# Opposite 64x64 corners for the join of a block inverse, with operands of two batches moved by DMA and the third projection placed ahead

## The reference, cut to what matters

```python
q = _causal_conv_silu(hidden_states @ Wq, conv_q)   # k, v alike, 16 heads, DK 96, DV 192
def step(S, inp):
    q_t, k_t, v_t, g_t, b_t = inp
    S = S * jnp.exp(g_t)[..., None, None]
    kv = jnp.einsum('bhk,bhkv->bhv', k_t, S)
    delta = (v_t - kv) * b_t[..., None]
    S = S + jnp.einsum('bhk,bhv->bhkv', k_t, delta)
    o = jnp.einsum('bhk,bhkv->bhv', q_t, S)
    return (S, o)
_, o = jax.lax.scan(step, S0, xs)
```

## Time and profile before

| | us |
|---|---|
| median of 3 runs | 2243.75 |
| lowest and highest | 2242.56, 2245.61 |
| the profiled execution, own time | 2241.96 |
| its span, first to last instruction | 2240.1 |

### The profile page before, as it was taken

How to read it: one execution, slowest core, us unless ns; L and a number is a source line. 1 busy time by engine, 2 the same in 40 slices (tenths; PEclk the granted TensorE clock), 3 DMA queues, 4 the chain that set the end, 5 groups by cost and what they waited for, 6 DMA issues and landing times. The chain is left out here.

```text
span 2240.1 us, 58394 instructions
## 1 busy us (share of the span) xinstructions
PE 2135.4 (95%) x21560; PEld 1489.9 (67%) x21560; DVE 1987.2 (89%) x4323; ACT 1373.8 (61%) x3891; POOL 1069.0 (48%) x1539
## 2 busy tenths in 40 slices
PE   5899999999999999999999999999999998868998
PEld 3576767676777776777767777767676766743544
DVE  8999999999999999999999999999999986467786
ACT  5566666666666667666766767666656554214655
POOL 2545454544545454545454545454545352125554
PEclk8999999999999999999999999999999998788999
DMA  5223333333333333334344433432222222140000
GB/s 143 51 69 80 78 82 80 85 84 85 85 80 85 74 84 90 94 87 94 89 94 92 95 91 95 93 76 66 66 62 51 58 51 55 28 164 9 20 24 29
DMA packets 455176, 169.16 MB, mean 76 GB/s; under 512 B 378310, under 2 KB 433894, under 8 KB 454380
## 3 DMA queue, kind: packets, MB, share of 16 engines
q1 hardware_dynamic: 454892, 165.43, 30.8%
HBM read 83.30 MB, written 56.90 MB: 63 GB/s over the span
## 5 line engine op out<-in xcount | busy, mean ns | idle before, releaser
L1491 DVE SCALAR_TENSOR_TENSOR d_y<-bank,d_cw,d_y 128x508 f32<-128x508 f32 (+2 forms) x576 | 421.3, 732 | 6.7 <-ACT d_y L1253 1.7
L851 POOL TENSOR_SCALAR d_ms<-d_sso 128x4 f32<-128x4 f32 x64 | 14.5, 226 | 531.6 <-ACT d_junk L1392 531.6
L799 POOL TENSOR_TENSOR d_Gm<-cst,gh 128x512 f16<-128x512 f32 x128 | 130.9, 1044 | 189.0 <-DVE d_ohl L1658 184.5
L1260 ACT ACTIVATE d_th<-d_y 128x512 f32<-128x512 f32 x192 | 121.0, 630 | 150.2 <-DVE d_y L1497 123.6
L1253 ACT ACTIVATE d_y<-bank,d_cw 128x512 f32<-128x512 f32 x192 | 130.7, 681 | 56.0 <-PE bank L917 53.7
L1664 DVE SCALAR_TENSOR_TENSOR x<-bank,x 128x512 f32<-128x512 f32 x128 | 87.0, 680 | 83.4 <-PE bank L1064 83.4
L834 POOL TENSOR_TENSOR d_V<-d_tok,d_kinv 128x640 f32<-128x640 f32 (+1 forms) x128 | 137.7, 1096 | 46.5 <-issue 44.0
L881 POOL TENSOR_SCALAR d_K<-d_tok,d_Em 128x96 f32<-128x96 f32 x256 | 155.9, 624 | 0.1
L1302 ACT ACTIVATE d_tok<-bank 128x384 f32<-128x384 f32 x256 | 125.5, 490 | 41.5 <-PE bank L933 37.7
L1382 ACT ACTIVATE d_Dl<-bank 128x384 f32<-128x384 f32 x128 | 62.2, 490 | 119.2 <-PE bank L1040 119.1
L1028 PE MATMUL bank<-d_wgh,hhi 128*128 128x192 f16 x1024 | 126.6, 246 | 0.0
(11 more groups left out here) (337 smaller groups left out, 6618.6 us busy)
## 6 DMA issues: line engine op xcount, KB each, us to landing
normed<-d_ohl SPq DMA_DIRECT2D x64, 384.0 KB, 3.7
lt_blocks<-d_LT SPq DMA_DIRECT2D x64, 256.0 KB, 2.6
d_fw<-turned_gate_w SPq DMA_DIRECT2D x32, 256.0 KB, 3.2
d_XT<-x_blocks SPq DMA_DIRECT2D x128, 64.0 KB, 2.4
d_X<-x_blocks SPq DMA_DIRECT2D x128, 64.0 KB, 2.5
d_fw<-turned_val_w SPq DMA_DIRECT2D x32, 256.0 KB, 3.2
d_fw<-turned_out_w SPq DMA_DIRECT2D x32, 256.0 KB, 2.8
d_st<-in_L_attn_Wg_dram SPq DMA_DIRECT2D x16, 384.0 KB, 4.1
```

The lines of the kernel that those rows point to most:

```text
L799: nc.gpsimd.tensor_tensor(Gm[:, w, :, :], over(U, 1, B), over(gh[:, w, n, :], 2, P), ALU.mult).then_inc(s["Gm_ready"], 1)
L1260: nc.scalar.activation(th[:, :, :], y[(st.p + j) % 2][:, :, :], ACT.Tanh).then_inc(s["tanh_done"], 1)
L1491: nc.vector.scalar_tensor_tensor(out=yy[:, :, tap:], in0=pp[:, :, 0:P - tap], scalar=cw[:, ds(st.kp, 1), t, 3 - tap], in1=yy[:, :, tap:], ...
```

## The change

- `y_join` and `x_join` do four matmuls of 64 rows and 64 columns each in place of four of 128 rows. Batches 0 and 1 use array rows 0 to 63 and write PSUM partitions 64 to 127; batches 2 and 3 use rows 64 to 127 and write partitions 0 to 63 (for `x_join` the other way round). The two kinds alternate in the instruction order. `x_join` writes the last quarter of bank 3.
- Operands of batches 2 and 3 are needed on the other 64 partitions. Three DMAs of 32 KB on SyncE's queue bring them in every step: LJ (from LT, `turned_join`), and XJ's two halves (from X and XT, `halves`).
- `turned_join` stands before `gather`, `halves` between `next_weights` and `store`. `y_join` waits for LJ and the first half of XJ, `x_join` for the second.
- `proj(2)` moves ahead of `y_join`: five of six parts for c > 0 (the sixth between the joins), all six for c = 0, with `turn(2)` among them. At c = 0 one output tile and `turn(3)` stand between the joins where there is one output unit; in steps 0, 4 and 60 nothing does.
- ScalarE copies the upper XT block first in `copy_x64`, `copy_yj` copies 128 partitions x 128 in place of 64 x 256, `join` is two copies of 64 x 128 in place of one of 64 x 256.

```diff
+            def turned_join(n, q):
+                past(sp, "x21_done", n)
+                past(sp, "LT_ready", B * n + B)
+                sp.dma_start(LJ[HB:P, :, :], LT[q][0:HB, 2:B, HB:P]).then_inc(s["LJ_in"], 16)
+            def halves(n):
+                past(sp, "X_ready", 7 * n + 5)
+                sp.dma_start(XJ[HB:P, :, :], X[0:HB, 0, 2:B, :]).then_inc(s["XJ_in"], 16)
+                past(sp, "X_ready", 7 * n + 6)
+                sp.dma_start(XJ[0:HB, :, :], XT[HB:P, 2:B, HB:P]).then_inc(s["XTJ_in"], 16)
...
             def y_join(st):
                 hold(pe, s["X_ready"], 7 * st.n + 7)
-                for i in range(B):
-                    last = nc.tensor.matmul(lev[HB:P, 2 * P + i * HB:2 * P + (i + 1) * HB], LT[st.p][:, i, HB:P], X[:, 0, i, :], start=True, stop=True)
+                past(pe, "LJ_in", 16 * st.n + 16)
+                past(pe, "XJ_in", 16 * st.n + 16)
+                for i in range(2):
+                    at = slice(2 * P + i * HB, 2 * P + (i + 1) * HB)
+                    nc.tensor.matmul(lev[HB:P, at], LT[st.p][0:HB, i, HB:P], X[0:HB, 0, i, :], start=True, stop=True)
+                    last = nc.tensor.matmul(lev[0:HB, at], LJ[HB:P, i, :], XJ[HB:P, i, :], start=True, stop=True)
                 last.then_inc(s["yps_done"], 1)
             def x_join(st):
                 hold(pe, s["Y_ready"], 2 * st.n + 2)
-                for i in range(B):
-                    last = nc.tensor.matmul(lev[0:HB, 2 * P + i * HB:2 * P + (i + 1) * HB], YJ[:, i, :], XT[:, i, HB:P], start=True, stop=True)
+                past(pe, "XTJ_in", 16 * st.n + 16)
+                for i in range(2):
+                    at = slice(3 * P + i * HB, 3 * P + (i + 1) * HB)
+                    nc.tensor.matmul(lev[0:HB, at], YJ[HB:P, i, :], XT[HB:P, i, HB:P], start=True, stop=True)
+                    last = nc.tensor.matmul(lev[HB:P, at], YJ[0:HB, i, :], XJ[0:HB, i, :], start=True, stop=True)
                 last.then_inc(s["x21_done"], 1)
...
-                    nc.scalar.activation(YJ[HB:P, :, :].rearrange("p b t -> p (b t)"), lev[HB:P, 2 * P:], ACT.Copy).then_inc(s["Y_ready"], 1)
+                    nc.scalar.activation(YJ[:, :, :].rearrange("p b t -> p (b t)"), lev[:, 2 * P:3 * P], ACT.Copy).then_inc(s["Y_ready"], 1)
...
-                    nc.scalar.activation(XT[0:HB, :, HB:P], lev[0:HB, 2 * P:].rearrange("p (b t) -> p b t", b=B), ACT.Copy).then_inc(s["XT_ready"], 1)
+                    for h in range(2):
+                        last = nc.scalar.activation(XT[0:HB, 2 * h:2 * h + 2, HB:P], lev[h * HB:(h + 1) * HB, 3 * P:].rearrange("p (b t) -> p b t", b=2), ACT.Copy)
+                    last.then_inc(s["XT_ready"], 1)
```

More of the change, by code:

```diff
@@ L92 @@
     L_moved rec_done Xb_ready X_stored XT_stored X_loaded block_in
+    LJ_in XJ_in XTJ_in
     ks_done qs_done W_ready qs_read yps_done Y16_ready Y_ready xps_done X_ready x21_done XT_ready
@@ L115, in delta_tiles @@
         "Y32": sb("Y32", [P, B, HB // 2]),
-        "YJ": sb("YJ", [P, B, HB]),
+        "YJ": sb("YJ", [P, 2, HB]),
         "X": sb("X", [P, 2, B, HB]),
@@ L625, in stage_delta_rule @@
         onT = [sb(f"onT{q}", [P, 2 * 6, P], F16) for q in range(2)]
+        LJ = sb("LJ", [P, 2, HB])
+        XJ = sb("XJ", [P, 2, HB])
         ones = sb("ones", [P, P])
@@ L776, in step @@
                     load_go(st.k + 1)
+                if st.recur:
+                    turned_join(st.n, st.p)
                 if st.turn:
@@ L780, in step @@
                         next_weights(i + 1)
+                if st.recur:
+                    halves(st.n)
                 if st.output:
@@ L1041, in pair_of, with output @@
                 last.then_inc(s[done], 1)
-            def output(st):
+            def output(st, lo=0, hi=4):
                 n = st.n
                 for e, u in enumerate(units(n)):
+                    if not lo <= 2 * e + 1 or not 2 * e < hi:
+                        continue
                     past(pe, f"onT_in{u % 2}", 16 * (u // 2 + 1))
@@ L1050, in output @@
                     for i in range(2):
+                        if not lo <= 2 * e + i < hi:
+                            continue
                         at = (6, 5, 7, 4)[2 * e + i]
@@ L1177, in step @@
                     proj(1, 5, 6)
-                    proj(2, 0, 6)
+                    for part in range(4):
+                        proj(2, part, 6)
+                    turn(2)
+                    proj(2, 4, 6)
+                    proj(2, 5, 6)
                 else:
@@ L1186, in step @@
                     proj(1, 5, 6)
+                    for part in range(5):
+                        proj(2, part, 6)
                 if n == NS - 1:
@@ L1190, in step @@
                 if c:
-                    proj(2, 0, 6)
+                    proj(2, 5, 6)
                 past(pe, "W_ready", B * n + 2)
                 pair_of(st, "qs_done", 0, 4, lambda i: qry[0:DK, i, :], lambda i: S[:, i, :], product=c > 0)
-                turn(2)
-                if c == 0:
-                    for part in (1, 2, 3):
-                        proj(2, part, 6)
+                if c:
+                    turn(2)
+                elif len(units(n)) == 1:
+                    output(st, 0, 1)
+                    turn(3)
                 x_join(st)
-                if c:
-                    proj(2, 1, 6)
                 past(pe, "PT_ready", n + 1)
                 pair_of(st, "qs_done", 1, 7, lambda i: qry[0:DK, i, :], lambda i: S[:, i, :], product=c > 0)
-                turn(3)
+                if c or len(units(n)) != 1:
+                    turn(3)
                 if n == NS - 1:
                     turn_x(1)
-                for part in range(4 if c == 0 else 2, 6):
-                    proj(2, part, 6)
-                if len(units(n)) < 2:
-                    output(st)
+                if len(units(n)) == 1:
+                    output(st, 0 if c else 1, 2)
                 if n == 0:
@@ L1335, in copy_x64 @@
                     nc.scalar.activation(X[32:HB, 0, :, 0:32], lev[32:HB, 0:P].rearrange("p (b e) -> p b e", b=B), ACT.Copy).then_inc(s["X_ready"], 1)
-                    for h in range(2):
+                    for h in (1, 0):
                         r = slice(h * HB, h * HB + 32)
```

## The result

The changed kernel takes 2257.5 us (median of 10 runs, 2251.9 to 2268.9), against 2243.6 for the kernel before beside it. The ratio is 1.0068, with a 95% interval of 1.0056 to 1.0081: 0.7% slower. 2226 was predicted. The profiled execution of the change took 2251.9 us and its span is 2250.1. That is 10.0 us more than the span before, so the trace shows some 10 of the 14 to 15 us; it is the fastest of the ten executions.

A forecast was written before the change was run, and what follows sets the result against it. PE's order was taken to bound most steps, VectorE's chain those of c = 0. Gains of 22.1 us less 4.5 for transfers made 17.6, giving 2226 us, with a range of 2212 to 2241.

The forecast's parts named there:

- The overlap of two 64x64 tiles: At y_join and x_join: a pair of tiles costs what one does, 0.48 us a step; no overlap had chance 0.10.
- the 22.1 of the sum: Gain over all steps before transfers: c = 1 8.2, c = 2 5.3, c = 3 7.2, last four steps 1.4 us.
- The moved projection: Ten matmuls ahead of y_join: PE's sum unchanged, ScalarE's list about 1.1 us later, nothing added; bounds 0 to 0.3 us.
- The 0 for c = 0 in the sum: Steps of c = 0: VectorE's chain to gate_pair(0) sets the time, so PE's savings there gain 0.
- The transfers: XJ behind the weight chunk on SyncE's queue: waits in about a dozen steps, priced 3 plus 1.5, together 4.5 us.
- XJ is late in every step: Rival at y_join: XJ arrives 1.4 us behind PE in 37 steps, 52 us less what hides, 2260 or more; chance 0.09.
- The clock rival: PE's longer gate wait at c = 0 lowers its clock: 13 steps lose 1.7 us each, 2248; chance 0.05.
- The signs: Prediction wrong if c = 3 is 29.0 or more, XJ waits exceed 0.3 us in most steps, or c = 0 under 26.7.
- the period still of 27.0 at c = 0: Profile after, steps of c = 0: PE waits about 1 us for the gate and the step length stays 27.0 us.

The follow-up runs named there:

- b_order: Kernel before with TensorE's new order alone (third projection ahead of y_join), old joins, no transfers: ratio 1.0064 to before.
- b_tiles: Kernel before with the paired 64x64 tiles and ScalarE's new copies, old order, constant operands for batches 2 and 3, no transfers: ratio 0.9895.
- b_order_best: b_order with GpSimd's multiply into V waiting for VectorE's last block instruction, and at c = 0 low_o ahead of it, waiting for silu(1): ratio 0.9980.
- b_hit: Kernel before with GpSimd's multiply into V also waiting for ScalarE's tanh(1), the event VectorE's silu(1) waits for: ratio 1.0071.
- b_late: Kernel before with GpSimd's multiply into V also waiting for VectorE's last block instruction of the step: ratio 0.9989.
- a_best: Changed kernel, XJ issued ahead of weight chunk, GpSimd's V multiply after VectorE's last block instruction, low_o ahead of it at c = 0: 2218.8 us, ratio 0.9901.
- a_halves: Changed kernel with SyncE issuing the two transfers into XJ ahead of the weight chunk instead of behind it: ratio 0.9993 to before.
- a_late: Changed kernel with GpSimd's multiply into V also waiting for VectorE's last block instruction of the step: ratio 1.0119 to before.

## Why the prediction was wrong

- **The overlap of two 64x64 tiles: right.** 0.48 us a step at c = 1 to 3 was forecast. c = 3 is at 28.55 in the undisturbed steps, 0.42 below before and 0.46 below b_order. The tiles alone gave 23 us for the 22.1 of the sum, but that agreement is partly luck: in b_tiles c = 1 gave 3.6 us in steps 6 to 59 where the sum has 8.2 for it, c = 2 gave 7.1 for 5.3, and c = 0 and steps 0 to 5 gave another 4.9 where it has about 1. A rule that spoke against it (the Trainium skill, TensorEngine Tiling (Array Packing), Restrictions and Gotchas: different row tiles cannot access the same PSUM bank simultaneously) is contradicted by pairs of row tiles that both write bank 3, start 0.00 to 0.04 us apart and, four pairs together, take 0.38 us to the next matmul instead of 0.61. The two tiles of a pair write different partitions of the bank; no run has two row tiles on the same ones.
- **"The moved projection", with "Nothing is added to the sum for these": the main step that failed.** I saw that `tokens(3)` and `tanh(1)` move back, and followed only `tanh(1)` to VectorE's list (14.0 us after `y_16` forecast at c = 1, 14.2 measured), with bounds of 0 to 0.3 us at c = 2 and 3. `tokens(3)` has a second reader, GpSimd's multiply, and I never asked when that would run or what runs on VectorE beside it. At c = 0 I did not work out the delay at all. It is 2.5 us there and not 1.1, because all of `proj(2)` stood between. The price is 14 us by b_order, of which b_order_best ties 8 to 9 to the multiply.
- **The 0 for c = 0 in the sum: right for what PE saves, blind to what VectorE can lose.** That VectorE's chain is the bound there means that PE's savings are worth nothing, but also that whatever lengthens a VectorE instruction on it costs in full. In the trace of before the collisions were visible, the same correction taking 0.17 or 0.54 us. b_hit shows that 0.94 us a step was at stake.
- **"The transfers", 4.5 us: too small by about four times in the queue's term.** I had XJ land 0.1 to 0.3 after the chunk, in time, with waits in about a dozen steps that add up to 5 us. XJ's 2.6 us from issue to landing is about what I had taken, but there were 22 waits, with 11.6 us, and one of about 0.4 at c = 0, where I counted none because PE has time there. It goes through `y_join`, `copy_yj`, `tokens(3)` and `tanh(1)` to VectorE. The place behind the chunk cost 17 us. The transfers by themselves cost 8.5 more by the medians, of which no trace shows how much is theirs. The rival "XJ is late in every step" (2260) did not occur: PE waited for XJ in 22 of 56 steps, and it landed 2.6 us after its issue, 3.5 at most. That the time fell near that rival's is luck. (Up to step 48 there are 36 steps with c > 0, not 37.)
- **The clock rival did not occur at c = 0.** The wait of 0.83 us left PEclk at 1.00 in the stretch above, and so it is in all steps from 6 to 59 of before and after. In steps 61 and 62 it was 0.96 and 0.74, against 1.00 and 0.80 before. The step length times what the clock lacks to 1 makes that 12.7 us for 8.5, an estimate, which is about the 3.9 us lost at the end. In step 61 PE had just waited 3.1 us for the transposed `onT`, where it was 1.3 before. Waits of 2.5 and 3.0 us there, with 0.96 and 0.95, stand in b_late and b_tiles too, which have no transfers, so the cause is open. Two of the change's ten executions, the slowest (2265 and 2269 us), had a mean of 0.971 and 0.970 where the traced one had 0.976.
- **The signs.** I had named three things that would make the prediction wrong: c = 3 at 29.0 or more, waits for XJ over 0.3 us in most steps, c = 0 under 26.7. None came. c = 3 was 28.73, XJ was waited for in 22 of 56 steps, and c = 0 went the other way, to 27.97; I had not named that it could become longer. Of what the profile after was to show, the period still of 27.0 at c = 0 is what failed, and it tells where to look.

## What to carry to other kernels

When an engine's order changes, list every reader of each result that becomes later, on every engine, and ask what each of them will then run beside; an idle-looking GpSimd can be the one that matters. Where VectorE sets the time, the start of a long GpSimd operation on SBUF is a scheduling decision like any other: put it beside VectorE instructions that read PSUM, as the runs with the moved multiply did. Small transfers that someone waits for go ahead of large ones that nobody waits for.

## What the runs showed of the hardware

- **VectorE and GpSimd take turns.** In step 32 after, GpSimd's first multiply runs 1017.99 to 1019.24, the silu, ready at 1018.40, takes 1.38 instead of 0.67 and ends 0.54 after it. In b_hit the silu is first and keeps its 0.69, and the next pair of VectorE instructions pays. It looks like waiting for a whole instruction and not like sharing. VectorE's convolution steps, which have one operand in PSUM, keep their 0.72 us beside the same multiply; in a_best it runs 1005.60 to 1007.21, with these on VectorE, of which only the last (both operands in SBUF) is lengthened, from 0.17:

```profile
1006.09 0.72 DVE L1533 SCALAR_TENSOR_TENSOR d_y<-bank,d_cw,d_y 128x500 f32<-128x500 f32 x1
1006.84 0.39 DVE L1539 TENSOR_TENSOR d_y<-d_y,d_corr 128x12 f32<-128x12 f32 x1
```

  The Trainium skill (SBUF — State Buffer, Who interferes with whom) says this: the port pair is an exclusive lock, which a VectorE operation with two SBUF inputs wants only against a GpSimd operation that reads SBUF. The traces agree in both points: 1.38 us for 0.67 with two SBUF inputs, 0.72 unchanged with one in PSUM. No run has a GpSimd operation beside it that only writes SBUF.
- **A 32 KB transfer behind a 256 KB one in the same queue** took 2.6 us from issue to landing (median), 3.0 and more in single steps, against 1.8 when it was issued ahead of the chunk (a_halves).
- **Two 64x64 tiles in opposite corners** run at the cost of one, writing different partitions of the same PSUM bank: four pairs in 0.38 us from the join to the next matmul, eight full-row passes in 0.61.
- **A PE wait of 2 to 3 us can cost more than itself.** In step 33 of a_late the granted clock went from 1.00 to 0.57 for 3.6 us right behind the wait of 2.54 us, with pieces at the lower level (1.2 GHz): two projection matmuls took 0.95 us there and 0.60 in after. It did not follow every such wait: step 25, with 2.59 us, kept 1.00.
